# A three-layer interaction network on one core: block 1's first layer moved behind block 0's, and block 0's second layer on whole matmuls

## The reference

```python
h = x                                        # x: (512, 39, 16)
for i in range(3):
    Wr = Ws[i].reshape(39, h.shape[1], 128)  # h.shape[1]: 39, 64, 64
    out = relu(einsum('bfd,bgd,fgs->bsd', x, h, Wr) + bs[i][None, :, None])
    if i < 2: h, direct = out[:, :64], out[:, 64:]
    else:     direct = out
    outs.append(direct)
return sum(concatenate(outs, axis=1), axis=-1)      # (512, 256)
```

## Time and profile before

| | |
|---|---|
| time, median of 3 runs | 584.98 us (584.91 to 585.09) |
| profiled execution | 584.89 us |
| its span, first to last instruction | 583.1 us |
| PE busy | 559.0 us (96%) |
| DVE, ACT, POOL busy | 536.2, 374.3, 514.0 us |
| mean granted clock of PE | 0.984 |
| moved by transfers | 121.69 MB, 209 GB/s |

### The profile page before, as it was taken

One profiled execution on the slowest core, in us unless ns is written; L12 is line 12 of the kernel. 1 busy time (PEld: TensorE's weight loads), 2 busy tenths in 40 slices (PEclk: granted clock), 3 DMA queues, 4 the chain that ended last, 5 costly groups with the idle time before them and its releaser, 6 DMA issues.

```text
span 583.1 us, 7873 instructions
## 1 busy us (share of the span) xinstructions
PE 559.0 (96%) x2029; PEld 383.8 (66%) x2029; DVE 536.2 (92%) x514; ACT 374.3 (64%) x419; POOL 514.0 (88%) x229
## 2 busy tenths in 40 slices
PE   3895999999999999999999999999999999999997
PEld 1363676767666676776666677676666767667765
DVE  3588989999999999999999999999999999999975
ACT  2476556576757667665766766666586676758562
POOL 0687959989898998989999898998989899898995
PEclk9796999999999999999999999999999999999999
DMA  8999734927558383755828366582846649162001
GB/s 332 420 417 346 276 109 118 346 78 269 215 166 325 98 324 118 245 223 177 327 79 318 142 218 250 158 343 68 308 166 191 277 139 348 65 215 97 0 2 37
DMA packets 26959, 121.69 MB, mean 209 GB/s; under 512 B 3264, under 2 KB 3392, under 8 KB 24768
## 3 DMA queue, kind: packets, MB, share of 16 engines
q1 hardware_dynamic: 26944, 121.52, 57.4%
HBM read 120.98 MB, written 0.52 MB: 208 GB/s over the span
## 4 chain that ended last, share of the span: by engine, by line
PE 86%; issue 4%; DMA 3%; DVE 3%; POOL 2%; ACT 2%; SPq 0%; POOLq 0%; DVEq 0%; ACTq 0%
PE acc L471 86%; DMA xfirst<-x 3%; POOL z_lo L234 2%; DVE z_raw L351 1%; DVE z_whole L351 1%; ACT z_hi L540 1%; ACT h L543 0%; ACT last L543 0%; DVE z_hi L232 0%; DVE z_psum L351 0%; DVE z_lo L234 0%; SPq L244 0%; ACT direct L543 0%; DVE sums L374 0%; DVE z_lo L231 0%
## 5 line engine op out<-in xcount | busy, mean ns | idle before, releaser
L234 POOL TENSOR_TENSOR z_lo<-z_raw,z_hi 128x1024 fp32r<-128x1024 f32 (+1 forms) x222 | 508.1, 2325 | 49.1 <-ACT z_hi L540 46.9
L540 ACT CAST z_hi<-z_raw 128x1024 fp32r<-128x1024 f32 (+1 forms) x222 | 223.4, 1019 | 116.3 <-DVE z_raw L351 83.7
L351 DVE TENSOR_TENSOR z_raw<-h,xwide 128x1024 f32<-128x1024 f32 x192 | 229.8, 1219 | 8.5 <-ACT h L543 7.4
L471 PE MATMUL acc<-z_hi,w_hi 128*128 128x512 f32 (+2 forms) x557 | 219.3, 463 | 7.7 <-ACT direct L543 6.9
L471 PE MATMUL acc<-z_hi,w_lo 128*128 128x512 f32 (+2 forms) x557 | 181.7, 396 | 0.0
L471 PE MATMUL acc<-z_lo,w_hi 128*128 128x512 f32 (+1 forms) x525 | 169.8, 397 | 1.3 <-POOL z_lo L234 1.1
L471 PEld LDWEIGHTS acc<-z_hi,w_hi 128*128 128x128 f32 (+2 forms) x557 | 105.1, 189 | 67.5 <-issue 40.0
L471 PE MATMUL acc<-z_whole,w_whole 128*128 128x512 f32 x256 | 124.6, 611 | 2.8 <-DVE z_whole L351 2.8
L471 PEld LDWEIGHTS acc<-z_hi,w_lo 128*128 128x128 f32 (+2 forms) x557 | 104.8, 188 | 28.2 <-issue 3.6
L471 PEld LDWEIGHTS acc<-z_lo,w_hi 128*128 128x128 f32 (+1 forms) x525 | 98.2, 188 | 27.4 <-POOL z_lo L234 3.3
L351 DVE TENSOR_TENSOR z_whole<-h,xwide 128x1024 f32<-128x1024 f32 x64 | 77.8, 1217 | 5.3 <-ACT h L543 5.3
(11 more groups left out here) (16 smaller groups left out, 91.4 us busy)
## 6 DMA issues: line engine op xcount, KB each, us to landing
xwide<-x SPq DMA_DIRECT2D x160, 512.0 KB, 4.7
xfirst<-x SPq DMA_DIRECT2D x15, 2048.0 KB, 7.7
xwide<-w SPq DMA_DIRECT2D x2, 1024.0 KB, 12.6
xfirst<-x SPq DMA_DIRECT2D x2, 768.0 KB, 6.0
xfirst<-x SPq DMA_DIRECT2D x1, 512.0 KB, 6.9
w_whole<-w_rest SPq DMA_DIRECT2D x1, 512.0 KB, 10.3
w<-w0a SPq DMA_DIRECT2D x1, 448.0 KB, 5.1
direct<-w0b SPq DMA_DIRECT2D x1, 448.0 KB, 6.1
```

The source lines that it names most:

```text
L234: return eng.tensor_tensor(lo[0:rows, 0:n, :], z[0:rows, 0:n, :], hi[0:rows, 0:n, :].bitcast(F32), ALU.subtract)
L351: nc.vector.tensor_tensor(dst, in0, in1, ALU.mult).then_inc(made[kind], 1)
L471: return nc.tensor.matmul(dst, w[0:rows, place, :], z[0:rows, t - G * g, :], start=first and first_g and t == G * g, stop=final and t == T ...
L540: nc.scalar.copy(z_hi[0:rows, slot("PV", pair, par, pos, HI_RING), 0:n, :], src).then_inc(hi_made, 1)
```

## The change

- Step 0 begins with block 1's layer 0, all four groups whole. Its x lands in a second place, `xsecond`, which lies over xwide's second half; DVE reads the replica of steps -1 and 0 from SBUF and not from PSUM.
- Layer 1 of block 0 follows, in the order 1, 3, 0, 2, 4, ... 9; groups 0 to 8 are whole, with the unsplit weights of `stage[1]` where a group is P or V otherwise, and group 9 stays V.
- Step 1 begins with layer 0 of block 2. Layer 2's weights are split within step 1: ACT before position 6, DVE before position 7. relu1 of block 0 is at position 4.
- The folding of w0 is done in two pieces, each with transfers of its own, the first ahead of x.
- DVE fills a tile with zeros, and PE works 14 matmuls on it before all else, into the accumulator of layer 2.
- SP's order follows. Two wide groups of block 1 wait for PE's last whole group of step 0, two for layer 2's low weights.

The diff, cut:

```diff
-FIRST_0 = (1, 3, 0, 2)
-SCHEDULE_0 = "111100001111112222222222"
-SCHEDULE_1 = "111222222211000011111222"
-RELU1_AT_1 = 3
+ORDER_1_0 = ((1, "W"), (3, "W"), (0, "W"), (2, "W"), (4, "W"), (5, "W"), (6, "W"), (7, "W"), (8, "W"), (9, "V"))
+SCHEDULE_1 = "000011111211222211212222"
+RELU1_AT_1 = 4
+SPLIT2_AT_1, LOW2_AT_1 = 6, 7
...
+WARM = 14
...
-         0: [(1, g, KINDS[1][g]) for g in FIRST_0] + steps(SCHEDULE_0)[len(FIRST_0):],
+         0: [(0, g, "W") for g in range(len(KINDS[0]))] + [(1, g, k) for g, k in ORDER_1_0],
...
+FOLD = (range(0, G), range(G, T0))
...
+        xsecond = xwide[:, 1, 0:1 + T0, :]
...
         def _(sp):
...
             def load_wide(j, half, g):
...
-            load_first(0, xfirst_head_in[0], range(0, 1 + G))
-            sp.dma_start(w0[:], w0a).then_inc(w0_in, 16)
-            sp.dma_start(w0t, w0b).then_inc(w0_in, 16)
+            for k, ts in enumerate(FOLD):
+                sp.dma_start(w0[:, ts[0]:ts[-1] + 1, :], w0a[:, ts[0]:ts[-1] + 1, :]).then_inc(w0_in[k], 16)
+                sp.dma_start(w0t[:, ts[0]:ts[-1] + 1, :], w0b[:, ts[0]:ts[-1] + 1, :]).then_inc(w0_in[k], 16)
+                if k == 0:
+                    load_first(0, xfirst_head_in[0], range(0, 1 + G))
...
+            load_first(1, xsecond_in[0], range(0, 1 + G), xsecond)
+            load_first(1, xsecond_in[1], range(1 + G, 1 + T0), xsecond)
+            load_wide(0, 0, ORDER_1_0[0][0])
+            sp.dma_start(w_whole[:], w_rest).then_inc(w_whole_in, 16)
+            load_wide(0, 0, ORDER_1_0[1][0])
...
-            sp.dma_start(w_whole[:], w_rest).then_inc(w_whole_in, 16)
-            for g in FIRST_0:
+            for g, _ in ORDER_1_0[2:]:
...
             sp.wait_ge(*made_all(-1, 0))
-            load_first(1, xfirst_in)
-            for g in range(4, 6):
-                load_wide(0, 0, g)
+            load_first(2, xfirst_in)
+            sp.wait_ge(*made_all(0, 0))
+            for g in range(2):
+                load_wide(1, 1, g)
...
-            for g in range(6, G12):
-                load_wide(0, 0, g)
-            for g in range(G12 - 4):
+            for g in range(2, G12 - 4):
...
-            sp.wait_ge(*made_all(0, 0))
-            load_first(2, xfirst_in)
...
+            sp.wait_ge(whole_used, before("W", 1, 0))
+            for g in range(G12 - 2, G12):
+                load_wide(1, 1, g)
...
-            for g in range(G12 - 4, G12):
+            for g in range(G12 - 4, G12 - 2):
...
                 refill(0, par)
...
-                    if g == 0:
-                        dve.wait_ge(xrep_ready, j + 2)
...
+                    elif isinstance(j, int) and j == 0:
+                        if g < len(xsecond_in):
+                            dve.wait_ge(xsecond_in[g], 16)
...
-                        dve.wait_ge(xfirst_in, 16 * (j + 2))
-                    in0 = xrep_psum[0:P0, None, :].to_broadcast([P0, n, N])
-                    in1 = xshift[:, G * g:G * g + n, :]
+                        dve.wait_ge(xrep_ready, j)
+                        dve.wait_ge(xfirst_in, 16 * (j + 1))
+                    if isinstance(j, int) and j < 1:
+                        tile = xfirst if j < 0 else xsecond
+                        in0 = tile[0:P0, 0:1, :].to_broadcast([P0, n, N])
+                        in1 = tile[0:P0, 1 + G * g:1 + G * g + n, :]
+                    else:
+                        in0 = xrep_psum[0:P0, None, :].to_broadcast([P0, n, N])
+                        in1 = xshift[:, G * g:G * g + n, :]
...
+                    if isinstance(j, int) and j == 1 and pos == LOW2_AT_1:
+                        a, n = SPLIT_FROM[2], SPLIT_COUNT[2]
+                        dve.wait_ge(w_hi_made, len(SPLIT0) + 2)
+                        nc.vector.tensor_tensor(w_lo[:, a:a + n, :], stage[2][:, 0:n, :],
+                                                w_hi[:, a:a + n, :].bitcast(F32), ALU.subtract).then_inc(w2_lo_made, 1)
...
+            def fold(k):
+                ts = FOLD[k]
+                dve.wait_ge(w0_in[k], 32)
+                part = w0[:, ts[0]:ts[-1] + 1, :]
+                nc.vector.tensor_tensor(part, part, w0t[:, ts[0]:ts[-1] + 1, :], ALU.add).then_inc(w0_folded, 1)
+            zero = z_whole[:, WHOLE_RING - 1, 0, :]
+            nc.vector.memset(zero, 0.0).then_inc(zero_set, 1)
+            dve.wait_ge(zero_set, 1)
+            nc.vector.tensor_copy(zeros[:], zero).then_inc(zeros_made, 1)
+            dve.wait_ge(zeros_made, 1)
+            fold(0)
             products(-1, 0, 0)
-            dve.wait_ge(w0_in, 32)
-            nc.vector.tensor_tensor(w0[:], w0[:], w0t, ALU.add).then_inc(w0_folded, 1)
+            fold(1)
...
             step(-1, 1)
-            a, n = SPLIT_FROM[2], SPLIT_COUNT[2]
-            dve.wait_ge(w_hi_made, len(SPLIT0) + 2)
-            nc.vector.tensor_tensor(w_lo[:, a:a + n, :], stage[2][:, 0:n, :], w_hi[:, a:a + n, :].bitcast(F32),
-                                    ALU.subtract).then_inc(w2_lo_made, 1)
...
                 def matmul(w, z, t, first, final):
...
-                    place = t if w is w0 else PLACE[layer, t]
+                    place = t if w is w0 else PLACE[layer, t] - (SPLIT_FROM[1] if w is stage[1] else 0)
...
+                    w = w0 if layer == 0 else w_whole
+                    if layer and KINDS[layer][g] != "W":
+                        pe.wait_ge(w_staged[1], 16)
+                        w = stage[1]
...
-                        mm = matmul(w0 if layer == 0 else w_whole, z, t, True, True)
+                        mm = matmul(w, z, t, True, True)
...
-                if isinstance(j, int) and j == 0:
-                    if layer == 0:
-                        pe.wait_ge(w_lo_made, len(SPLIT0))
-                    else:
-                        pe.wait_ge(w1_lo_made, 1)
+                if isinstance(j, int) and (layer, j) == (0, 1):
+                    pe.wait_ge(w_lo_made, len(SPLIT0))
+                if isinstance(j, int) and (layer, j) == (1, 0):
+                    pe.wait_ge(w1_lo_made, 1)
...
+            pe.wait_ge(zeros_made, 1)
+            for _ in range(WARM):
+                nc.tensor.matmul(acc[2][:, :], zeros[:, 0:SIZE], zeros[:], start=True, stop=True)
...
-            step(-1, 0)
+            contract(-1, 0, 0)
+            pe.wait_ge(w0_folded, 2)
+            for pos in range(1, len(order(-1))):
+                contract(-1, 0, pos)
...
             step(-1, 1)
...
             def copy_xrep(j):
-                if isinstance(j, int) and j == -1:
-                    act.wait_ge(xfirst_head_in[0], 16)
-                else:
-                    act.wait_ge(xfirst_in, 16 * (j + 2))
-                if not isinstance(j, int) or j >= 0:
+                act.wait_ge(xfirst_in, 16 * (j + 1))
+                if not isinstance(j, int) or j > 1:
...
-                    if (layer, g) == (0, 0) if isinstance(j, int) and j == 0 else \
-                            pos == XREP_AT and has(0, BLOCKS - 2):
+                    if pos == XREP_AT and has(2, BLOCKS - 2):
...
-                    if isinstance(j, int) and j == 0 and (layer, g) == SPLIT2_BEFORE:
+                    if isinstance(j, int) and j == 1 and pos == SPLIT2_AT_1:
...
+                    copy_xrep(1)
...
             def split(raw, a, n, rows):
...
-            copy_xrep(-1)
-            act.wait_ge(w0_folded, 1)
+            act.wait_ge(w0_folded, 2)
...
-            split_layer(1)
...
+            split_layer(1)
             step(-1, 1)
...
```

More of the change, by code:

```diff
@@ L129 @@
 SPLIT0 = [(PLACE[0, tiles_of(0, g)[0]], tiles_of(0, g)) for g, k in enumerate(KINDS[0]) if k != "W"]
-SPLIT2_BEFORE = (1, 6)
+FOLD = (range(0, G), range(G, T0))
+assert sorted(g for g, _ in ORDER_1_0) == list(range(G12))
 assert len(SPLIT0) > 0 and SPLIT_COUNT[1] <= 16 and SPLIT_COUNT[2] <= 16
@@ L157, in cin @@
         z_lo = sb("z_lo", [128, LO_RING, G, N], F32R)
+        zeros = sb("zeros", [128, N], F32R)
         direct = sb("direct", [128, 2, N])
@@ L170, in cin @@
                  xwide[:, 1, T12 - 8:T12 - 4, :].rearrange("p a (b s) -> p (a b) s", s=SIZE)]
+        xsecond = xwide[:, 1, 0:1 + T0, :]
         w0t = direct[:].rearrange("p a (b s) -> p (a b) s", s=SIZE)[:, 0:T0, :]
-        w0_in = sem("w0_in")
+        w0_in = [sem("w0_in0"), sem("w0_in1")]
         w0_folded = sem("w0_folded")
@@ L183, in cin @@
         xfirst_head_in = [sem("xfirst_head_in0"), sem("xfirst_head_in1")]
+        xsecond_in = [sem("xsecond_in0"), sem("xsecond_in1")]
         xw_in = [[sem(f"xw_in{p}_{g}") for g in range(G12)] for p in range(2)]
@@ L193, in cin @@
         summed = sem("summed")
+        zero_set = sem("zero_set")
+        zeros_made = sem("zeros_made")
         out_sent = sem("out_sent")
@@ L240, in _, with load_first @@
         def _(sp):
-            def load_first(j, landed, slots=range(1 + T0)):
+            def load_first(j, landed, slots=range(1 + T0), tile=xfirst):
                 src = bass.AP(x0.tensor, x0.offset + 128 * (1 + T0) * N * j + N * slots[0],
```

(2 more changed lines are left out.)

## The result

| | before | after |
|---|---|---|
| time, median | 584.94 us (584.57 to 585.09, 4 runs) | 579.39 us (579.33 to 580.32, 4 runs) |
| ratio, 95% interval | | 0.991 (0.9893 to 0.9927) |
| profiled execution | 584.89 us | 579.43 us |
| its span | 583.1 us | 577.3 us |
| PE busy | 559.0 us | 562.6 us |

A forecast was written before the change was run, and what follows sets the result against it. PE bounds the body, so only the start can shrink: an earlier start of step 1, less 5.6 us of stalls, ends it at 80.0 instead of 87.94. That is -7.9 us, giving 577.1 us, range 573.5 to 581.0.

The forecast's parts named there:

- step 1's end decides: Whole change: its worth is how much earlier PE ends step 1, forecast 80.0 against 87.94, 7.9 us.
- the zeros matter little: Kernel start: zeros that do not wake the clock slow groups 0 and 1 by 1.7 us, costing nearly nothing.
- PE goes on at 17.1: Behind block 0's first layer: PE restarts at 17.1 after waiting for all three activations, a 2.2 us hole.
- Group 1's data at 9.0 and group 2's at 11.06, as before: Block 0's first layer: these landings bind and stay unchanged; PE ends the layer near 14.9 instead of 16.8.
- The clock in the third pause: PE's pause from 14.9 to 17.1: the forecast expected no lasting half speed, as PE has no pause afterwards.
- Rival D: Start: the clock falls in the 2.2 us pause and stays down through step 0, giving 593.5 us; chance 0.05.
- End of step 0 39.6: Step 0: PE is the bound, working 22.5 us from 17.1 without a gap; before, this work ended at 43.9.
- xfirst lands at 37.4 and sets step 1's start: Step 1's start: block 2's xfirst lands at 37.4, then ACT's copy and activations let PE start at 40.1.
- PE may slip by 3.1 us for free: Step 0's end: PE may slip from 39.6 to 42.75, when relu1 wants it, without moving the end.
- The chain in step 1: Step 1: late weight split, DVE's subtraction (ending 50.45) and POOL's low parts stall PE 5.6 us; end 80.0.
- The whole groups: Step 0, layer 1: seven groups made whole cost PE 0.31 us more each, 2.2 us.
- The body: Bytes, tail and loop after the start: same bytes, same code, so no change in time.

The follow-up runs named there:

- e2: The changed kernel without the 14 matmuls on zeros (DVE's fill and copy stay); 579.70 us.
- e8: The changed kernel with w0's folding in one piece again and block 0's first x ahead of it in the queue; 579.11 us.
- e1: The changed kernel with PE's wait for w_rest moved from ahead of step 0 to layer 1's first group; 578.69 us.
- e10: The changed kernel again, unedited, in the same rounds as a later edit; 580.20 us.
- e7: e6 with layer 2's split weights loaded behind block 0's last wide group, split by ACT at step 0's end and DVE ahead of step 1's first product; 577.07 us.
- e5: e1 plus nine matmuls on zeros behind block 0's layer 0, filling PE's pause; 577.98 us.
- e6: e1 with block 1's layer 0 accumulating in layer 2's accumulator, so PE need not wait for block 0's activations; 577.63 us.
- e4: The changed kernel with layer 2's split weights loaded behind layer 1's and split in step 0 (ACT position 4, DVE position 10); 577.02 us.
- e3: The changed kernel with layer 1 of block 0 keeping its kinds P, W and V, so split as before; 580.01 us.

## Why the prediction was right, and where it was wrong

The time lies in the range and the sign is right. Some luck is in it: PE's end of step 0 was 4.15 us late, of which 3.0 reached the end of step 1, and 0.95 us that were not forecast came back in step 2. That step 1's end decides and that the zeros matter little (e2) held. The steps:

- **"PE goes on at 17.1"**: 19.32. Half of the 2.2 us is the end of block 0's layer 0: ACT's activations began at 16.15, where the forecast implies 15.07. "Group 1's data at 9.0 and group 2's at 11.06, as before" was wrong, since w0 in two pieces put two more issues ahead of them (e8): they landed at 9.84 and 11.74. The other 0.4 us is small gaps and the last matmul's end, which I took from starts of matmuls and not from the row's end. The other half, 1.1 us, is PE's wait for w_rest, that stands ahead of step 0 in the code: before the change nobody noticed, since layer 1's groups needed these weights anyway. I had even worked out their landing (18.6) and not asked who waits for it.
- **The clock in the third pause.** Rival D had the place right: in the trace of the change it fell there and rose before 23, which cost 1.7 us. The pause had grown to 3.27 us, but the forecast length of 2.2 was no protection: e1, with 2.19, lost the clock in three runs of four. D's own mechanism, half speed through the whole of step 0, did not come; the stretches of half speed in the profiles were 3.4 us long here and 6.8 in e10 and e7 (43.1 to 49.9 us).
- **"End of step 0 39.6"**: 43.75, the sum of both and of 0.2 us of small waits.
- **"xfirst lands at 37.4 and sets step 1's start"**: in the change it was there before ACT asked (no wait at 39.41). DVE's first product of step 1 came at 40.85 instead of 38.0, because DVE is tied to PE by the ring of four whole products (its product at 35.98 waited 0.49 us for PE's read of an old one, as those ahead of it do), so PE's lateness went straight into it. Where PE was earlier the landing did bind, at 38.81 in e5 and 38.26 in e6. e6 comes nearest to the timing that I had forecast: PE ends step 0 at 39.1 (39.6), xfirst lands at 38.26 (37.4), step 1 ends at 81.05 (80.0). So with PE in time the sum would have been 1.05 us short, most of it the landing.
- **"PE may slip by 3.1 us for free"**: wrong in the change for that reason. It slipped by 4.15, and step 1's end by 3.0 (83.03 against 80.0). I had looked at relu1's need of PE, not at the ring.
- **The chain in step 1**: right, 2.8 us late. PE's losses were 5.0 us, forecast 5.6; the subtraction ended at 53.22, forecast 50.45. DVE's subtraction began while POOL worked until 51.06 and ended 2.16 later, at 53.22; POOL's next one, begun at 51.42, took 4.04 us instead of 2.33 and so ended 2.24 behind DVE's end. That is what the Trainium skill states in "SBUF — State Buffer", section "Who interferes with whom"; the trace agrees, in both directions. With POOL idle beside it the same subtraction of DVE takes 2.28 us (e4).
- **The whole groups**: 2.2 us dearer in step 0, as forecast, but not a net cost: kept split they would have cost PE 4.0 us of waits there (e3). The prediction has no term for that.
- **The body**: forecast nothing, measured 0.95 us for, in step 2, and 0.3 against, outside the span.

Mis-sized in sum: 3.0 us at step 1's end, less 0.95, plus 0.3, is 2.4; the profiled execution fell by 5.46 where 7.9 was forecast.

## What to carry to other kernels

When an order is changed, walk each engine's waits in their place in the code, not only the waits that the moved work needs: a wait that was free where it stood may now stand ahead of work that doesn't need it. Before work is moved to a place where the other engines are in a hurry (here the weight split), look for idle time that it could use instead. Engines coupled by a ring of a few buffers share their lateness. And a cure for a visible stall, such as a low clock, is worth only what the next bound leaves: compare the start of the chain, here a landing, before adding it.
